# A transformer block on one core: projection stage laid out in slots, residual rows formed in the output stage

## What is computed

```python
h = layernorm(x) * (1 + ca) + sa                 # first normalisation, then modulation per batch
xn = layernorm(h) * gamma + beta                 # second normalisation
q, k = rope(xn @ Wq + bq), rope(xn @ Wk + bk);  v = xn @ Wv + bv
att = softmax(causal(q @ k.T / 4)) @ v           # 16 heads of 16
x = x + ga * (h + att @ Wo + bo)                 # h, not x, is the inner residual
# then an expert layer on the first 2048 rows, with its own modulation and gate
```

## Time and profile before

| | |
|---|---|
| runs, median (lowest to highest) | 3243.47 us (3242.13 to 3244.9) |
| profiled execution, its own time | 3240.84 us |
| its span | 3239.1 us |
| busy share of the span: TensorE, VectorE, ScalarE, GpSimd | 87%, 70%, 54%, 29% |
| mean granted TensorE clock (1 is 2.4 GHz, 0.5 is 1.2 GHz) | 0.935 |
| bytes moved by DMA | 402.96 MB |

### The profile page before, as it was taken

How to read it: one execution, slowest core, us unless ns; L and a number is a source line. 1 busy time by engine, 2 the same in 40 slices (tenths; PEclk the granted TensorE clock), 3 DMA queues, 4 the chain that set the end, 5 groups by cost and what they waited for, 6 DMA issues and landing times. The chain is left out here.

```text
span 3239.1 us, 48169 instructions
## 1 busy us (share of the span) xinstructions
PE 2817.5 (87%) x17587; PEld 1353.4 (42%) x17587; DVE 2278.7 (70%) x3286; ACT 1765.1 (54%) x3595; POOL 948.2 (29%) x1174
## 2 busy tenths in 40 slices
PE   1677777775999999999999999999999879975997
PEld 0333333331444444444444444444444347753664
DVE  4899999986777777777777777777777435553231
ACT  1455555550777777777777777777777721111111
POOL 2677777762112221121222211212222100003231
PEclk7888888885999999999999999999999989987999
DMA  2355555547344444445444444444444146663332
GB/s 77 127 192 192 192 192 192 191 156 169 71 97 96 92 93 91 99 100 100 97 94 92 94 91 100 100 100 97 91 94 93 42 188 258 258 230 102 79 103 54
DMA packets 173951, 402.96 MB, mean 124 GB/s; under 512 B 33147, under 2 KB 85792, under 8 KB 157107
## 3 DMA queue, kind: packets, MB, share of 16 engines
q1 hardware_dynamic: 167572, 391.36, 46.0%
q0 software_dynamic: 6144, 8.52, 1.5%
HBM read 240.65 MB, written 161.31 MB: 124 GB/s over the span
## 5 line engine op out<-in xcount | busy, mean ns | idle before, releaser
L962 DVE TENSOR_REDUCE mx<-ps 128x2 f32<-128x1024 f32 (+3 forms) x1216 | 1371.4, 1167 | 396.8 <-PE ps L1050 301.6
L1008 ACT ACTIVATE prob<-ps 128x512 f32<-128x512 f32 (+1 forms) x2560 | 1252.0, 560 | 538.4 <-PE ps L1068 529.7
L1043 PE MATMUL ps<-k_rows,q_rows 96*128 96x512 bf16 (+3 forms) x3072 | 911.2, 332 | 38.1 <-DMA k_rows<-k_parts 31.4
L1068 PE MATMUL ps<-q_rows,k_rows 99*128 99x512 bf16 (+3 forms) x3072 | 907.2, 328 | 14.7 <-ACT prob L1008 6.1
L901 POOL TENSOR_SCALAR_AFFINE_SELECT prob<-prob 128x512 f32<-128x512 f32 x512 | 320.0, 637 | 1451.3 <-ACT prob L1008 1451.3
L1087 PE MATMUL ps<-prob,v_rows 128*32 128x512 f32 (+3 forms) x6144 | 628.2, 496 | 0.0
L1068 PEld LDWEIGHTS ps<-q_rows,k_rows 99*128 99x128 bf16 x3072 | 273.1, 98 | 599.0 <-ACT prob L1008 360.2
L1043 PEld LDWEIGHTS ps<-k_rows,q_rows 96*128 96x128 bf16 x3072 | 290.2, 98 | 268.5 <-DVE mx L962 60.7
L1050 PE MATMUL ps<-mask_b,unit_b 128*128 128x128 bf16 (+2 forms) x1408 | 348.6, 248 | 0.0
L701 PE MATMUL ps<-x_t,w_all 128*128 128x512 f32 x512 | 233.2, 598 | 23.2 <-ACT x_t L582 23.2
L1087 PEld LDWEIGHTS ps<-prob,v_rows 128*32 128x32 f32 x6144 | 134.3, 108 | 245.8 <-ACT prob L1008 122.9
(11 more groups left out here) (154 smaller groups left out, 2745.3 us busy)
## 6 DMA issues: line engine op xcount, KB each, us to landing
k_rows<-k_parts SPq DMA_DIRECT2D x384, 128.0 KB, 7.4
v_ones<-v_st SPq DMA_DIRECT2D x64, 512.0 KB, 9.2
v_rows<-v_ones SPq DMA_DIRECT2D x64, 512.0 KB, 9.3
att<-o_sb SPq DMA_DIRECT2D x128, 256.0 KB, 3.2
att_b<-att SPq DMA_DIRECT2D x16, 2048.0 KB, 9.8
q_parts<-stage SPq DMA_DIRECT2D x128, 192.0 KB, 3.6
k_parts<-stage SPq DMA_DIRECT2D x128, 192.0 KB, 3.2
q_rows<-q_parts SPq DMA_DIRECT2D x64, 384.0 KB, 4.5
```

The costliest lines, as they stand in the source:

```text
L962: dve.tensor_reduce(dst, src, AX.X, ALU.max).then_inc(a_free, 1)
L1008: nc.scalar.activation(prob[:, (g * NPC + i) % RING, h, 0:w], src, ACT.Exp).then_inc(exp_done, 1)
L1043: ins = pe.matmul(ps[:, at, col:col + w], q[0:ROWS, g, h, i * P:(i + 1) * P], k[0:ROWS, g, h, k0:k0 + w], start=(r == 0), stop=True, skip_ ...
L1068: ins = pe.matmul(ps[:, PS_B + bank(g, n), at:at + w], k[0:AUG, g, h, j * P:(j + 1) * P], q[0:AUG, g, h, q0:q0 + w], start=True, stop=True)
```

## The change

In the projection stage the step list becomes a list of slots `s` from -19 to 127, eight per batch, of which the even ones project. An operation of a later batch stands in slot `s` by its lead: loads and statistics of x 19 slots ahead, first normalisation 14, GpSimd 13, second statistics 12, second normalisation 4, transposes one slot after that. GpSimd does both the multiplication and the addition of the shift (VectorE still adds it for batch 0). The residual is no longer formed or stored there; `xin` and `mods` are rings of three; the first normalisation is written over `xin`; and the two statistics `rsx` and `nmx` of all batches are kept until the output stage. There Sync loads `x` and the row `M_A2` instead of the residual, ScalarE normalises tile t of batch b+1 ahead of its copy of tile t of batch b, and GpSimd multiplies and adds.

```diff
         @block.sync                                  # phase1
             def load(b):
-                reuse(sp, r_done, b * T - T)
-                reuse(sp, h_done, b * T - T)
-                sp.dma_start(xin[:, p], ...)
-            def store_residual(b):
-                sp.wait_ge(r_done, b * T + T)
-                sp.dma_start(resid_d[b], h1[:, b % 2]).then_inc(r_stored[b % 2], DMA)
+                r = b % RING
+                if b == RING:
+                    sp.wait_ge(first_done, T)
+                elif b > RING:
+                    sp.wait_ge(h_done, (b - RING) * T)
+                sp.dma_start(xin[:, r], ...)
...
+        START = -19
+        def batch_at(s, lead):
+            b, k = (s + lead) // T, (s + lead) % T
+            return (b, k) if 0 <= b < B else (None, None)
+        def normed_in(s):
+            b, k = batch_at(s, 4)
+            if b is not None and k < 6:
+                yield ((0, 1), (2, 3), (4,), (5,), (6,), (7,))[k], b
+        def turned_in(s):
+            return normed_in(s - 1)
...
         @block.vector
-            def shift_h(b, tiles): ...
+            def slot(s):
+                if s >= 0 and s % 2 == 0:
+                    multiply(s // 2)
+                if s >= 0 and s % 2 == 1:
+                    if s > 1:
+                        take_rest(s // 2 - 1)
+                    combine(s // 2)
+                b, k = batch_at(s, 14)
+                if b is not None and k == 0:
+                    invert_x(b)
+                b, k = batch_at(s, 4)
+                if b is not None and k == 0:
+                    invert_h(b)
+                b, k = batch_at(s, 12)
+                if b is not None:
+                    take_h(b, k)
+                    if k == T - 1:
+                        join_h(b)
+                b, k = batch_at(s, 19)
+                if b is not None and k < 4:
+                    take_x(b, k)                      # two tiles
+                    if k == 3:
+                        join_x(b)
         @block.scalar
+            def slot(s):
+                b, k = batch_at(s, 14)
+                if b is not None and k == 0:
+                    root(b, 0, agx, agx_done, sdx_done)
+                b, k = batch_at(s, 4)
+                if b is not None and k == 0:
+                    root(b, 1, agh, agh_done, sdh_done)
+                if s > 0 and s % 2 == 0:
+                    high(s // 2 - 1)
+                if s >= 0 and s % 2 == 1:
+                    for t in (s % T - 1, s % T):
+                        copy_v(s // T, t)
+                    if s > 1:
+                        middle(s // 2 - 1)
+                for tiles, b in turned_in(s):
+                    for t in tiles:
+                        copy_x(b, t)
+                b, k = batch_at(s, 14)
+                if b is not None:
+                    first_norm(b, k)
+                for tiles, b in normed_in(s):
+                    for t in tiles:
+                        second_norm(b, t)
         @block.gpsimd
-            def residual(b, tiles): ...
+            def modulate(b, t):
+                pool.wait_ge(h1_done, b * T + t + 1)
+                pool.tensor_tensor(h[:, p, t, :], xin[:, r, t, :], mods[:, r, M_CA1, :], ALU.mult).then_inc(h_mul, 1)
+                if b > 0:
+                    pool.wait_ge(h_mul, b * T + t + 1)
+                    pool.tensor_tensor(h[:, p, t, :], h[:, p, t, :], mods[:, r, M_SA, :], ALU.add).then_inc(h_done, 1)
+            def slot(s):
+                b, k = batch_at(s, 13)
+                if b is not None:
+                    modulate(b, k)
+                if s >= 4 and s % 2 == 0:
+                    low(s // 2 - 2)
         @block.tensor
+            def slot(s):
+                for tiles, b in turned_in(s):
+                    for t in tiles:
+                        turn_x(b, t)
+                if s >= 0 and s % 2 == 0:
+                    project(s // 2)
+                if s >= 0 and s % 2 == 1:
+                    for t in (s % T - 1, s % T):
+                        values(s // T, t)
...
         def load(sp, b, p):                          # phase3
             sp.dma_start(att[:, p], att_d[b].rearrange("g p t -> p g t")).then_inc(att_in[p], DMA)
-            sp.dma_start(res[:, p], resid_d[b]).then_inc(res_in[p], DMA)
+            reuse(sp, r_done, b * T - T)
+            sp.dma_start(xb[:, p], x[b].rearrange("(t p) d -> p t d", p=P)).then_inc(x_in[p], DMA)
+            sp.dma_start(a2[:, p], mods_d[b, M_A2, :].partition_broadcast(P)).then_inc(x_in[p], DMA)
...
         @block.scalar
+            def first_norm(b, t):
+                p = b % 2
+                if t == 0:
+                    act.wait_ge(x_in[p], (b // 2 + 1) * 2 * DMA)
+                    reuse(act, x2_done, b * T - T)
+                nc.scalar.activation(res[:, p, t, :], xb[:, p, t, :], ACT.Identity, bias=nmx[:, b, t:t + 1],
+                                     scale=rsx[:, b, t:t + 1]).then_inc(r_norm, 1)
             def work(b, half, p):
                 for t in range(T):
+                    if b + 1 < B:
+                        first_norm(b + 1, t)
                     act.wait_ge(nt_done, b * T + t + 1)
                     reuse(act, c_done, b * T + t - 1)
                     nc.scalar.copy(n_t[:, t % 2], ...).then_inc(nt_copied, 1)
+            for t in range(T):
+                first_norm(0, t)
             loop(act, work)
+        @block.gpsimd
+            def residual(b, t):
+                pool.wait_ge(r_norm, b * T + t + 1)
+                pool.tensor_tensor(res[:, p, t, :], res[:, p, t, :], a2[:, p, :], ALU.mult).then_inc(r_mul, 1)
+                pool.wait_ge(r_mul, b * T + t + 1)
+                pool.tensor_tensor(res[:, p, t, :], res[:, p, t, :], xb[:, p, t, :], ALU.add).then_inc(r_done, 1)
```

More of the change, by code:

```diff
@@ L512, in take_rest @@
                 dve.tensor_tensor(rest[:, n % 2], qr[:, n % 2], parts(n, 0), ALU.subtract).then_inc(rest_done, 1)
-            def both(nx, fr, bk, j):
-                n = bk * NP + j // 2
-                if fr is not None and j == 0:
-                    invert_x(fr)
-                if fr is not None and 1 <= j <= 4:
-                    shift_h(fr, (2 * j - 2, 2 * j - 1))
-                if fr is not None and j == 5:
-                    join_h(fr)
-                if fr is not None and j == 6:
-                    invert_h(fr)
-                if j % 2 == 0:
-                    multiply(n)
-                else:
-                    if n:
-                        take_rest(n - 1)
-                    combine(n)
-                if fr is not None and 1 <= j <= 4:
-                    take_h(fr, (2 * j - 2, 2 * j - 1))
-                if nx is not None and j in (5, 6):
-                    take_x(nx, range(4 * (j - 5), 4 * (j - 5) + 4))
-                if nx is not None and j == 7:
-                    join_x(nx)
@@ L551, in _ @@
+            dve.memset(eps[:, :], EPS)
+            for s in range(START, B * T):
+                slot(s)
             take_rest(B * NP - 1)
@@ L639, in _ @@
+            act.wait_ge(ones_set, 1)
+            for s in range(START, B * T):
+                slot(s)
             high(B * NP - 1)
@@ L712, in values @@
                 ins.then_inc(v_done, 1)
-            def both(nx, fr, bk, j):
-                if j % 2 == 0:
-                    project(bk, bk * NP + j // 2)
-                else:
-                    for t in (j - 1, j):
-                        values(bk, t)
-                if j in (0, 1):
-                    for t in (4 + 2 * j, 5 + 2 * j):
-                        turn_x(bk, t)
-                if fr is not None and j >= 6:
-                    for t in (2 * j - 12, 2 * j - 11):
-                        turn_x(fr, t)
-            for t in range(4):
-                turn_x(0, t)
-            steps(both)
+            def slot(s):
[7 more added lines that the diff above has]
+                        values(s // T, t)
+            for s in range(START, B * T):
+                slot(s)
 def phase2(nc, B, L, ps, ident, mask, q_d, k_d, v_d, max_d, att_d):
@@ L1189, in work @@
                 ins.then_inc(wg_done, 1)
-                dve.wait_ge(res_in[p], half * DMA + DMA)
                 for t in range(T + 2):
```

207 lines of the change are left out of this document (66 added, 141 removed).

## The result

The changed kernel takes 3654.66 us (median of 4 runs, 3652.5 to 3655.7) against 3243.3: the ratio is 1.1267, with a 95% interval of 1.1248 to 1.1287. That is 411 us slower. The profiled execution has a span of 3653.4 us at a mean granted clock of 0.88, against 3239.1 us at 0.935. The forecast was 3630, with a range of 3450 to 3715.

The account below looks back on a forecast made before the run. VectorE was taken to bound the projection stage and TensorE the output stage. 3240.8 + 180 for the projection stage + 208 for the output stage = 3629, given as 3630 us; eight in ten between 3450 and 3715.

Parts of the forecast that it names:

- The ring of the projection stage: Odd slots: projection, multiply, take_rest, middle, second_norm, transpose and next projection wait in turn; 45.2 us per batch against 40.96.
- The clock: Projection stage: TensorE's clock falls in three longer idle gaps per batch, 2.4 us each, 7.1 us, making 52.3 per batch.
- M4 to M6: From the start of VectorE's multiply for slot 4's projection to slot 6's: 14.9 us, or 17.3 with a clock fall.
- M6 to M0: From the start of multiply for slot 6's projection to the next batch's slot 0: 11.2 us, 13.6 with a fall.
- M0 to M2: From the start of multiply for slot 0's projection to slot 2's: 11.8 us, 14.2 with a fall.
- The ends of the stage: Projection stage: last batch 24.4 us against 18.9, +5.5; normalising tiles 0 to 5 ahead of projection 0, some +3.
- The output stage: ScalarE waits for x of the next batch, delaying TensorE's first product 12.1 us, plus a 2.4 clock fall; +208 in all.
- The shift on GpSimd: Projection stage: GpSimd's added shift contends with VectorE; 0.7 us per batch taken, bounded at 2.5.
- M2 to M4: From the start of multiply for slot 2's projection to slot 4's: 7.3 us, including 0.7 for contention.
- The rule named in the prediction: VectorE instructions with two SBUF inputs and GpSimd instructions reading SBUF exclude each other; M2 to M4 up to 2 us longer.
- The residual's removal: Projection stage: removing GpSimd's residual and its store gains nothing, since they lie beside VectorE's work.
- Rival 4: Normalisation fully ahead, VectorE the bound at 30 us per batch, x loaded in time: 3076 us, chance 0.05.

Follow-up runs that it names:

- two local corrections: Changed kernel with TensorE's project or values ahead of turn_x, and x and M_A2 in three buffers loaded one batch earlier: 3128.36 us, ratio 0.9636.

## Why the prediction was right, and where its sizes were off

- **The ring of the projection stage** is as described. The run with extra matmuls gives its length near full clock, 45.7 against 45.2; the two runs that reorder one list each open it at the two places named (`turn_x` ahead of the projection on TensorE, `second_norm` behind `middle` on ScalarE).
- **The clock** was the mis-sized term. I took three falls of 2.4 per batch and left the 3.0 us ahead of tile 3's transpose out. There the clock had fallen already, in the 5.70 us before, and it stayed low until 517, over the values and the second gap. So M4 to M6 took 19.43 instead of 17.3. Against the run with extra matmuls the low clock cost 2.4 in M6 to M0, 2.1 in M0 to M2 and 4.0 in M4 to M6 (15.4 there on average), where I had 2.4 for each; over all batches it is at least 8.3 per batch, not 7.1. On average a batch took (903.94 - 94.09) / 15 = 54.0, the last and the first project of slot 0: 25 us more for 15 of them than at the forecast 52.3, and that is nearly the whole distance from 3630 to 3655. The range reached to four falls of 2.8.
- **The ends of the stage**: ahead of projection 0 it was 3.2 (forecast 3); the last batch took 22.7 from its first to its last project (forecast 24.4), as its two gaps were only 3.04 us each: behind the first the projection took 4.72 us, behind the second 3.60. Together the stage lost 204 us instead of 180.
- **The output stage** lost 208 us, as forecast. By its parts: batch 0 had 15.0 us from the first transpose to the first product instead of 7.6, +7.4 (forecast 6); the other 14 have (208 - 7.4) / 14 = 14.3 each (forecast 14.5). That the sum comes out to the microsecond is luck: errors of mine cancel. ScalarE was released 13.9 us after the store on average and not 13.5, the product came 12.5 later and not 12.1, and what remains for the clock's fall is 1.8 and not 2.4.
- **The shift on GpSimd**: the contention was bounded at 2.5 per batch and taken as 0.7, and M2 to M4 was 7.70 against 7.3: there the two halves of `combine` took 1.21 each instead of 0.68, 1.1 in all. In M6 to M0 and M0 to M2, where VectorE idles 6.5 and 6.9 us, none of it shows: near full clock they took the 11.2 and 11.8 forecast. With the stalls gone it takes back 2.7 us per batch of the 3.4 that the move gives, and all of them once VectorE is the bound. The rule named in the prediction, by which the case for moving the shift would be weaker, is borne out by these later runs.
- **The residual's removal** is worth nothing, as forecast. The reason I gave, that VectorE bounds the projection stage of before and GpSimd's residual lies beside its work, is not borne out: without the residual VectorE had 32 us less to do, so it did hold VectorE up, and what its removal gave was lost again to the clock. What bounds the stage wasn't isolated; the order of its lists, with the 11.06 us idle of TensorE, is what the slots, once corrected, replaced with success.
- **Rival 4**, that the change does what its slots suggest, gave 3076. It is the idea of the change, and it is sound: with two local corrections it measures 3128. Of the 52 us between them some 40 are the projection stage, whose batch takes 32.6 on average and not 30 (it became 124 us shorter, from 634.6 to 510.6, and not 165), and 9 the output stage, 279.7 instead of 270.8. VectorE's own 30.4 in a batch include its waiting for GpSimd, which I had left out, and the other 2.7 are the stall in M4 to M6.

What would have shown me wrong didn't come: batches closer than 41 us, or ScalarE waiting on TensorE in the output stage.

## What to carry to other kernels

When work is laid out in slots, check inside each slot, not only between slots, that no engine's list puts work that is needed next behind a wait for this slot's result; a lead of 14 slots is worth nothing if the last step stands one slot ahead and behind `middle`. When a consumer is moved one batch forward (here the normalisation of b+1 in the list of b), its load and its buffer must move forward too. And an addition moved from VectorE to GpSimd is not free for VectorE while both read SBUF: compare the busy time of VectorE, not its number of instructions.

## What the runs showed of the hardware that I had not expected

- The issue of `a_b`, a row of 256 values spread over 128 partitions, held Sync's queue for 4.58 us behind the attention rows and x (median of 16: 4.4), and 1.43 ahead of the attention rows (median 1.46). Its length alone costs nothing: with x one batch earlier it took 4.1 us (median) and no stall was left. That the descriptors queued ahead make it wait is my reading; it wasn't tried alone.
- The granted clock stayed at 0.50 for 17 us across work, a gap of 2.94 us and more work, although the work between the gaps lasted 5.8 us (503.09 to 508.9). After a single gap it came back 4.8 us after work resumed; in the projection stage of before without the residual, after single gaps of 10.1 us, it came back 6.8, 7.4 and 11.4 us after.
- Filling idle time of TensorE with useless matmuls made the kernel 116 us faster. The edit takes away no work and no wait, and the granted clock of 300 us of the stage was 0.98 with it, against 0.73 for the stage without.
- An instruction of eight columns on VectorE takes 0.17 us or up to 1.81, by whether GpSimd is in the middle of a 128x1024 one.
